# A recommender tower in float32: 256 of its 780 pair products with samples on partitions, summed along the free axis

## What is computed

```python
e = jnp.stack([tbl_0[ids[:, 0]], ..., tbl_39[ids[:, 39]]], axis=1)   # 2048 x 40 x 64
vi, vj = e[:, i_idx, :], e[:, j_idx, :]          # np.triu_indices(40, k=1): 780 pairs
viW = jnp.einsum('bpd,pde->bpe', vi, W)          # W: 780 x 64 x 64
z = jnp.einsum('bpe,bpe->bp', viW, vj)
h = jnp.concatenate([z, dense_ctx], axis=1)      # 2048 x 796
h = jnp.maximum(h @ W_top1 + b_top1, 0.0)        # 512
h = jnp.maximum(h @ W_top2 + b_top2, 0.0)        # 256
y = h @ W_top3                                   # 1
```

## Time and profile before

| | us |
|---|---|
| median of three runs (1374.18 to 1374.57) | 1374.25 |
| the profiled execution | 1374.48 |
| its span, from the first to the last instruction | 1372.7 |
| TensorE busy | 1307.9 |
| VectorE busy | 928.9 |
| GpSimd busy | 604.8 |
| ScalarE busy | 83.4 |

### The profile page before, as it was taken

One profiled execution on the slowest core, in us unless ns is written; L12 is line 12 of the kernel. 1 busy time (PEld: TensorE's weight loads), 2 busy tenths in 40 slices (PEclk: granted clock), 3 DMA queues, 4 the chain that ended last, 5 costly groups with the idle time before them and its releaser, 6 DMA issues.

```text
span 1372.7 us, 17118 instructions
## 1 busy us (share of the span) xinstructions
PE 1307.9 (95%) x7024; PEld 463.4 (34%) x7024; DVE 928.9 (68%) x804; ACT 83.4 (6%) x137; POOL 604.8 (44%) x646
## 2 busy tenths in 40 slices
PE   0699999998999999999999999999999999999998
PEld 0233333332333333333333333333333333333333
DVE  0378877776634788788854588878873478888860
ACT  0000000000000000000000100000000000000001
POOL 6777777777777777754543444451000000000000
PEclk9899999999999999999999999999999999999999
DMA  4233332222222233322211222222110011111100
GB/s 163 42 73 73 70 69 73 73 66 65 65 42 58 66 74 72 74 66 63 65 45 37 47 66 62 62 64 53 47 40 23 23 48 51 50 47 47 32 1 0
DMA packets 49782, 77.38 MB, mean 56 GB/s; under 512 B 13540, under 2 KB 13540, under 8 KB 49576
## 3 DMA queue, kind: packets, MB, share of 16 engines
q1 hardware_dynamic: 29216, 55.26, 13.6%
q0 software_dynamic: 20480, 21.01, 8.4%
q10 hardware_dynamic: 8, 0.01, 0.0%
HBM read 76.22 MB, written 0.01 MB: 56 GB/s over the span
## 4 chain that ended last, share of the span: by engine, by line
PE 86%; POOL 9%; issue 3%; DMA 1%; ACT 1%; POOLq 0%
PE u_ps L311 48%; PE z_ps L328 25%; POOL rows L268 9%; PE turn_ps L342 6%; PE turn_ps L294 3%; PE turn_ps L347 2%; PE u_ps L342 1%; PE u_ps L313 1%; PE u_ps L347 1%; PE turn_ps L351 0%; DMA rows<-in_tbl,ids_all 0%; ACT h_sb L418 0%; DMA ids_all<-in_ids 0%; PE u_ps L351 0%; ACT y_row L424 0%
## 5 line engine op out<-in xcount | busy, mean ns | idle before, releaser
L388 DVE TENSOR_TENSOR prod<-u_ps,x 128x1024 f32<-128x1024 f32 x800 | 928.2, 1218 | 401.8 <-PE u_ps L313 398.4
L313 PE MATMUL u_ps<-x,w_ring 64*128 64x512 f32 x1600 | 759.9, 610 | 0.0
L311 PE MATMUL u_ps<-x,w_ring 64*128 64x512 f32 x1600 | 759.9, 610 | 0.0
L268 POOL DMA_INDIRECT rows<-in_tbl,ids_all x640 | 604.1, 944 | 326.9 <-issue 196.1
L311 PEld LDWEIGHTS u_ps<-x,w_ring 64*128 64x128 f32 x1600 | 279.9, 187 | 420.4 <-issue 324.9
L328 PE MATMUL z_ps<-prod,ones 128*32 128x512 f32 x3200 | 393.4, 601 | 0.0
L313 PEld LDWEIGHTS u_ps<-x,w_ring 64*128 64x128 f32 x1600 | 279.8, 187 | 0.0
L328 PEld LDWEIGHTS z_ps<-prod,ones 128*32 128x32 f32 x3200 | 85.6, 109 | 279.7 <-issue 152.4
L294 PE MATMUL turn_ps<-ident,rows 128*128 128x128 f32 x320 | 53.9, 293 | 60.3 <-DMA rows<-in_tbl,ids_all 54.3
L407 ACT COPY x<-turn_ps 128x512 f32<-128x512 f32 x80 | 46.9, 586 | 635.8 <-PE turn_ps L294 635.8
L342 PE MATMUL turn_ps<-z_sb,mlp_sb 128*128 128x512 f32 x182 | 81.5, 599 | 0.8 <-ACT z_sb L412 0.8
(11 more groups left out here) (19 smaller groups left out, 14.7 us busy)
## 6 DMA issues: line engine op xcount, KB each, us to landing
w_ring<-in_w_pair SPq DMA_DIRECT2D x200, 256.0 KB, 2.7
rows<-in_tbl,ids_all POOLq DMA_INDIRECT x640, 2.5
mlp_sb<-in_mlp SPq DMA_DIRECT2D x1, 2308.0 KB, 11.5
ids_all<-in_ids SPq DMA_DIRECT2D x1, 320.0 KB, 3.3
z_sb<-in_dense_t SPq DMA_DIRECT2D x4, 32.0 KB
out_y<-y_row ACTq DMA_DIRECT2D x4, 2.0 KB
```

The source lines that it names most:

```text
L268: nc.gpsimd.indirect_dma_start(rows[:, slot, s, par * DIM:(par + 1) * DIM], None, tables[f], bass.IndirectOffsetOnAxis(ap=ids_all[:, SUB * ...
L311: pe.matmul(u_ps[:, bank, :], w_ring[0:DIM, c % W_SLOTS, cols], x[0:DIM, b % 2, n_even, :], start=True, stop=True)
L313: pe.matmul(u_ps[:, bank + 1, :], w_ring[DIM:P, c % W_SLOTS, cols], x[DIM:P, b % 2, n, :], start=True, stop=True).then_inc(mains_done, 1)
L388: nc.vector.tensor_tensor(prod[:, full % PROD_SLOTS], u_ps[:, bank:bank + 2, :], other, ALU.mult).then_inc(prods_done, 1)
```

## The change

256 of the 780 pairs, those of duos 4 to 19 with the eight fields of duos 0 to 3, are computed in another arrangement, as "moving" units (kind R); there are 16 duos times 4 pieces of 128 samples, 64 such units in a block, in the place of the 64 units (n, 0) to (n, 3). The others are "standing" units (F and D), 136 in a block, and unchanged. In a moving unit the samples stand and the weights move: x of 128 samples (64 rows by 128 columns) stands in the array and eight fields' weights (64 x 512) move, once per half, so u_ps holds 128 samples by 2 x 512. VectorE multiplies by the rows of duos 0 to 3 as they were gathered, which are kept in a buffer of their own (kept). The sum over d now runs along the free axis, into zb (128 samples by 256 pairs):

- on ScalarE for three units of four: 16 activations (Copy) of 128x64, each with an accumulated column;
- on VectorE for the first 24 moving units of the program and every fourth of the later ones: one reduction of 128x1024 to 128x16, issued after the next unit's product.

Two "zr" events per block turn zb into z_sb (four 128x128 pieces each, through turn_ps); layer 1 has seven chunks as before, five from the standing units and two from the moving ones. Beside this: x has 28 slots in one ring instead of two blocks of 20; rows have six slots instead of ten; the weight ring is split into four groups for standing and three duos for moving units; sums of a group come three units after its last; the moving units are spread between the standing ones; the duos are placed anew (12 of the next block's in this block) and the dense layers' turns stand at units 16, 22, 28, 34, 40, 46 and 52 of the next block; layer 1 takes chunk five last, and layer 2 waits for each part of layer 1 at its own chunk.

```diff
-W_SLOTS = 8
-ROW_SLOTS = 10
+X_SLOTS = 28
+WF_SLOTS, WR_SLOTS = 4, 3
+ROW_SLOTS = 6
 U_SLOTS = 3
-PROD_SLOTS = 2 * GROUP
+FPROD_SLOTS, RPROD_SLOTS = 2 * GROUP, 4
+SUM_LAG = 3
...
+def block_units(b):
+    moving = [("R", n, s) for n in range(KEEP, DUOS) for s in range(SUBS[b])]
+    out, f, r = [], 0, 0
+    while f < NF or r < len(moving):
+        reach = DUOS if f >= NF else STANDING[f][1]
+        due = f >= NF or (r < len(moving) and f >= 8 and r * (NF - 20) <= (f - 8) * len(moving)
+                          and moving[r][1] <= reach)
+        if due:
+            out.append(moving[r])
+            r += 1
+        else:
+            out.append(STANDING[f])
+            f += 1
+    return out
...
+def on_vector(u):
+    r = R_AT[u]
+    return r < 24 or r % 4 == 3
...
+MLP_AT = {3: ("zr", 0), 5: ("zr", 1), 16: ("l1", 0), 22: ("l1", 1), 28: ("l1", 2), 34: ("l1", 3),
+          40: ("l2", 0), 46: ("l2", 1), 52: ("l3", 0)}
...
+                for half in range(2):
+                    on = slice(half * DIM, (half + 1) * DIM)
+                    if kind == "R":
+                        op = pe.matmul(u_ps[:, bank + half, :], x[on, x_slot(b, n), k * P:(k + 1) * P],
+                                       wr_ring[on, c % WR_SLOTS, :], start=True, stop=True)
...
+                    nc.vector.tensor_tensor(rprod[:, r % RPROD_SLOTS], u_ps[:, bank:bank + 2, :],
+                                            kept[:, b % 2, k:k + 1, :].to_broadcast([P, 2, KEPT * DIM]),
+                                            ALU.mult).then_inc(prods_done, 1)
...
+                nc.vector.tensor_reduce(zb[:, s, at:at + 2 * KEPT],
+                                        rprod[:, r % RPROD_SLOTS].rearrange("p h (j d) -> p (h j) d", d=DIM),
+                                        AX.X, ALU.add).then_inc(vsums_done, 1)
...
+            def sum_over_d(u):
+                b, _, n, s = ALL[u]
+                slot = R_AT[u] % RPROD_SLOTS
+                act.wait_ge(prods_done, u + 1)
+                at = (n - KEEP) * 2 * KEPT
+                for j in range(2 * KEPT):
+                    one = rprod[:, slot, j // KEPT, j % KEPT * DIM:(j % KEPT + 1) * DIM]
+                    op = nc.scalar.activation(one, one, ACT.Copy, accum_out=zb[:, s, at + j:at + j + 1])
+                op.then_inc(asums_done, 1)
```

More of the change, by code:

```diff
@@ L58, in pair_index, with last_use @@
+V_SUMS = [u for u in R_UNITS if on_vector(u)]
+A_SUMS = [u for u in R_UNITS if not on_vector(u)]
+V_AT = {u: i for i, u in enumerate(V_SUMS)}
+A_AT = {u: i for i, u in enumerate(A_SUMS)}
+def last_use(b, n):
+    return max(UNIT0[b] + q for q, (kind, m, k) in enumerate(UNITS[b])
+               if n == m or (kind != "R" and n == k))
 def pair_index(i, j):
@@ L132 @@
[L132 to L140, removed]
-            order += [("duo", *d) for d in duos.get(q, [])]
[L142 to L152, removed]
-    return order
@@ L156, in dlrm_tower @@
[L156 to L161, removed]
+        for n in range(EARLY_DUOS, DUOS):
+            at.setdefault(max(0, min(first[n] - 3, 8 + 7 * (n - EARLY_DUOS))), []).append((b, n))
+    if b + 1 < NB:
+        free = 116 if b == 0 else 70
+        for n in range(EARLY_DUOS):
+            at.setdefault(free + (len(UNITS[b]) - 4 - free) * n // EARLY_DUOS, []).append((b + 1, n))
@@ new lines, in duos_before_unit, with work_order @@
+    return at
+MLP_AT = {3: ("zr", 0), 5: ("zr", 1), 16: ("l1", 0), 22: ("l1", 1), 28: ("l1", 2), 34: ("l1", 3),
+          40: ("l2", 0), 46: ("l2", 1), 52: ("l3", 0)}
+def work_order():
+    order, sums = [], []
+    for b in range(NB):
+        duos = duos_before_unit(b)
+        for q in range(len(UNITS[b])):
+            u = UNIT0[b] + q
+            while sums and sums[0][0] <= u:
+                order.append(("sum", *sums.pop(0)[1:]))
+            order += [("duo", *d) for d in duos.get(q, [])]
+            if b and q in MLP_AT:
+                order.append((MLP_AT[q][0], b - 1, MLP_AT[q][1]))
+            order.append(("unit", b, u))
+            f = F_AT.get(u)
+            if f is not None and f % GROUP == GROUP - 1:
+                sums.append((u + 1 + SUM_LAG, b, f // GROUP - GROUPS * b))
+    order += [("zr", NB - 1, c) for c in range(ZR)]
+    order += [("sum", *s[1:]) for s in sums]
+    order += [(what, NB - 1, m) for what, m in MLP_AT.values() if what != "zr"]
+    return order
@@ L162, in dlrm_tower @@
+def dlrm_tower(nc, dense_t, ids, tables, mlp_w, w_standing, w_moving, out, N_DENSE):
+    order = work_order()
+    turn_at = {ev: t for t, ev in enumerate(ev for ev in order if ev[0] in ("duo", "zr", "l1", "l2", "l3"))}
     first_tail = turn_at["l1", NB - 1, 0]
+    for at, ev in enumerate(order):
+        if ev[0] == "duo" and DUOS * ev[1] + ev[2] >= X_SLOTS:
+            old = divmod(DUOS * ev[1] + ev[2] - X_SLOTS, DUOS)
+            assert ("unit", old[0], last_use(*old)) in order[:at], ev
@@ L295, in duo @@
+                pe.wait_ge(landed, total)
+                for s in range(SUBS[b]):
+                    op = pe.transpose(bank[:, s * P:(s + 1) * P], of[:, s, :], ident[:])
                 op.then_inc(turned, 1)
[L297 to L303, removed]
-                    pe.wait_ge(turn_read, turn_at["duo", b, n] + 1)
[L306 to L314, removed]
+            copied = set()
@@ L395, in _ @@
+            due = []
+            for what, b, u in order:
+                if what == "unit":
+                    products(u)
+                    if due:
+                        sum_over_d(due.pop())
+                    if u in V_AT:
+                        due.append(u)
+            for u in due:
+                sum_over_d(u)
         @block.scalar
@@ L433, in _ @@
                     duo(b, n)
+                elif what == "unit" and n in A_AT:
+                    sum_over_d(n)
+                elif what == "zr":
+                    move_zr(b, n)
                 elif what == "sum":
```

340 lines of the change are left out of this document (228 added, 112 removed).

## The result

The changed kernel takes 1377.7 us (median of ten runs, 1376.3 to 1380.6) against 1374.4 us: a ratio of 1.0025, interval 1.0015 to 1.0034. The prediction was 1352 us. It is 26 us too low, and the kernel is a little slower, not faster.

The account below looks back on a forecast made before the run. TensorE was taken to bound the kernel: 1374.5 - 122 (TensorE) + 6 (start) + 48 (VectorE) + 45 (ScalarE, waits at the bank) = 1352 us. Own range 1325 to 1366 us (45%); overall range 1318 to 1500 us.

Parts of the forecast that it names:

- What bounds the kernel before: Whole kernel: TensorE bounds it, busy 95% of the span with 86% of the chain, so a saving counts one for one.
- TensorE, -122: TensorE's own work: sums of 256 units go (131 us), eight turns of z are added (6 us); 122 us less.
- the start, +6: Start of the program: about 16 us more waiting for duos' gathers, about 9 us of later waits gone; net +6 us.
- VectorE, +48: Moving units on VectorE: 82 added reductions at 1.13 us each and their unevenness give back 48 us.
- ScalarE's price: ScalarE's sums of moving units: one 128x64 activation with accumulated column every 0.24 us, a burst of 16 3.84 us.
- t: Pitch of one of ScalarE's summing activations, taken as 0.24 us, between 216 ns with overlap and 316 ns without.
- Waits at the bank, +45: Dense turns: TensorE waits for the turn bank, whose reader on ScalarE stands behind bursts; 45 us added.
- The step that failed: Dense turns: waits of 5.4, 6.2 and twice 2.5 us, 16.7 us a block over three blocks, priced at their length.
- the first two terms: TensorE's saved work, -122 us, and added waiting for gathers at the start of the program, +6 us.
- A: Rival: ScalarE becomes the bound, slower than before, total crossing 1374 us at t about 0.295; chance 33%.
- the range given for t from 0.27 to 0.30 us: Case between forecast and ScalarE as the bound, by the pitch of ScalarE's activations: 1366 to 1383 us, chance 8%.

Follow-up runs that it names:

- the light kernel: Held-bursts kernel with reductions cut to 1 of 16 columns, moving units' products to 128x512 and bursts to 8 activations: 1268.3 us.
- the held bursts: Changed kernel with ScalarE's bursts held back by two units, the same instructions otherwise: 1317.1 us.
- the first two experiments: Both against the changed kernel: ScalarE's bursts held back by two units, 1317.1 us; waits before dense turns filled with overwritten products on TensorE, 1359.7 us.
- the second experiment: Changed kernel with TensorE's waits before the dense turns filled with products whose results are overwritten: 1359.7 us.

## Why the prediction was wrong

- **What bounds the kernel before**: right. The change and the experiments are read in the same units (0.853 us a unit, 1.85 us the sums of a group, 0.78 us a turn), and they fit.
- **TensorE, -122, and the start, +6**: right in direction, together 10 us short: the light kernel is 106 us under the kernel before, not 116. In its trace TensorE is busy 1197.2 us against 1307.9, 110.7 less, and waits 38.2 + 25.8 = 64.0 us for gathers against 54.3, 9.7 more. In the changed kernel itself the waits for gathers went as told: they last until 105.55 us, duo 9, and were placed at 107.
- **VectorE, +48**: the reduction's price was right, 1.13 us from start to start, and the size is borne out in part. The reductions cost 26 us. The 49 us between the light kernel and the held bursts also hold the narrower products and the shorter bursts, so that they agree with 48 is no clean test.
- **ScalarE's price**: t = 0.24 us, measured 0.24. It came from adding the price of a 128x1 operand (102 ns) and one overlap of 100 ns to 214 ns; in fact the activation follows the last read after 0.09 us and the read follows after 0.15. The sum of two guesses was right, but neither of its parts is shown; that is luck. The Trainium skill's figures without an accumulator ("ScalarE: Activation LUTs", What ACT_TABLE_LOAD costs) give an estimate of 146 ns, which agrees with the 0.15 us from the activation to its read; the 0.09 us from the read to the next activation come on top. The 240 ns estimated from the Trainium skill's cycles ("VectorE: DVE Perf Modes", The TRN2 errata) agree with the 241 ns that one activation lasts; the pitch is 0.24 us too, but as the sum of these two steps.
- **Waits at the bank, +45**: right; 42.6 us by the first two experiments, 41.9 by the waits in their traces, and the single waits within 0.2 us.
- **The step that failed** is the one that let a wait cost its own length: "It waits 5.4 us ... 16.7 us a block". Nine of the twelve waits, 2.39 to 6.01 us long, cost 1.6 to 2.5 us each beyond themselves, because the granted clock fell to its lower level and stayed there into the work behind. That is 18.0 us of the 26 by the second experiment. The trace of before had it: it shows no such wait in mid-program, but its start has waits for gathers, and the turns of the earlier trace rows take 1.09 us behind the 5.50 us wait at 45.72 and 0.63 behind the 3.70 at 55.73 (there the clock fell behind the turn, 0.60 on the mean from 56 to 60 us). I read these rows for the distance of the gathers alone. The Trainium skill, "TensorE: Matmul & The Clock Gate", Part 1, says that "the default state is throttled, and activity releases the throttle"; the trace agrees, with 0.50 in the stretches of waiting and just after.
- **The other 8 us** of the miss are the 10 of the first two terms, with 1 more for VectorE and 2 less for the waits at the bank. About 4 of the 10 are waits for gathers (9.7 against 6). TensorE's own time fell 11 us less than the 122 forecast, and the waits for ScalarE's reads, 8.4 us in the kernel before and 2.7 in the light one, hide 6 of what is missing. Why TensorE's time fell less stays open. The differences -106.1 + 48.8 + 42.6 + 18.0 give the 3.3 us measured, but they must: each is the step from one measured kernel to the next, so their sum checks nothing.
- **Rivals**: A, ScalarE as the bound, did not happen; it was idle 255.9 us waiting for products. The outcome fell into the range given for t from 0.27 to 0.30 us (1366 to 1383, 8%), but t was 0.24: the time came about by a mechanism that neither the forecast nor a rival held. The sign was missed with it: 26 us were more than the 22 forecast as the gain.

## What to carry to other kernels

An engine with room to spare can still be late: where it also reads a buffer that the bound engine needs back, put that read ahead of long work in its queue, not behind. Reordering alone, the same instructions, was worth 60 us here, more than the 22 that the whole change was forecast to bring. When pricing a wait of TensorE, look in the trace for work behind a wait of that size and take its longer duration; here nine of twelve cost 1.6 to 2.5 us extra. And a gain that moves from TensorE to two other engines has to be priced by where their instructions stand in the queues. Over the span neither was near its limit (74% and 55%), though VectorE was busy 92.6 of the 100 us from 500 to 600.

## What the runs showed of the hardware

- An activation with an accumulated column shows as two instructions, 241 and 187 ns long, that start 0.15 and 0.09 us apart in turn; 128x64 with its sum is 0.24 us.
- A reduction of 128x1024 to 128x16 in float32 from SBUF takes 1.21 us, one every 1.13 us between products, the price of a product of 128x1024.
- Work put into a wait pays for itself: 24 us more of products ended the program 18 us earlier.
- A wait of 3.02 us and one of 5.36 us were followed by nearly the same loss (7.81 and 7.91 us for a turn of 6.28).
- Of two waits of 2.39 us in the same block, one was followed by a granted clock of 0.55 and a turn of 5.40 us instead of 3.70, the other by a clock of 1.00 and a turn of the usual 1.88.
